# Two-layer graph network on one core: x's first tile at the head of SP's DMA queue, two x loads behind ACT's table load, one leading matmul fewer

## The chip, the cores and the metric

One core of one Trainium2 chip. The metric is the device time of one execution in microseconds; several executions are made and their median is given.

## What is computed

For each of 8 graphs there are x (1024 nodes by 256 features, float32) and a dense adjacency matrix adj (1024 by 1024). Two layers follow each other:

```python
deg = sum(adj, -1);  agg = einsum('bij,bjf->bif', adj, x) / maximum(deg, 1e-6)
x = layernorm(x + relu(concat([x, agg], 2) @ W.T))
Ah = adj + eye;  dh = rsqrt(sum(Ah, -1));  An = dh[:, :, None] * Ah * dh[:, None, :]
x = layernorm(x + relu(An @ x @ kernel + bias))
```

## The kernel before

Every matrix product is made of three TensorE products of rounded parts: each float32 operand a is split into a_hi, a rounded copy, and a_lo = a - a_hi, and hi·hi, lo·hi and hi·lo are summed in PSUM. So before TensorE can use a tile, one engine must copy it (ACT, at the start also DVE) and DVE must subtract.

The work is a loop over the 8 graphs. A graph's 1024 source nodes are 8 tiles j of 128, held on the partitions; a product gathers over j into PSUM banks 128 x 512. While one graph is worked on, the inputs of the next are loaded. SP issues nearly all loads and stores, in the order of its program, and waits only where a buffer must first come free.

The change touches only the start, before the first graph's gather. There the inputs come tile by tile:

- **SP (lines 230 to 241)** loads adj's tile 0 (`raw[:, 0, 0]`, 256 KB), adj's tile 1, and then for i = 1 to 3 a pair of x tiles (256 KB) and the two adj tiles of that pair, 256 KB each. W, the transposed x and the next rows of adj follow.
- **ACT (lines 502 to 517)** loads x's tile 0 (128 KB, `x0_loaded`) and x's tile 1 (128 KB, `x_first_loaded[0]`), loads its activation table (line 504), and then copies, in this order: the left half of adj's tile 0; x's tile 1; adj's tile 1; and for each later pair x's pair, the first adj tile, the second adj tile. Each copy waits for its own load. These copies go through one helper, so they all show line 313.
- **DVE (lines 828 to 858)** fills some constants, then copies the right half of adj's tile 0 (834), copies x's tile 0 (837), subtracts for x's tile 0 (839), for adj's tile 0 (842), for x's tile 1 (845), adj's tile 1 (847) and so on. The subtractions show line 547.
- **TensorE (`gather_start`, lines 914 to 952)** runs WARM leading matmuls on a constant tile (256 columns each, result never read), and then for each j six matmuls of 512 columns: two x_hi·adj_hi (line 936), two x_lo·adj_hi (945), two x_hi·adj_lo (949). The first two of j = 0 wait for x's tile 0 copied and both halves of adj's tile 0 copied; the next two for x's subtraction; the last two for adj's. The first two of j = 1 wait for x's tile 1 and adj's tile 1 copied, and so on. All copies run on the same in-order engines, so the order of the list above is the order in which they can be served.

In what follows adj tile 0, adj tile 1, x tile 0, x tile 1 and x pair 1 (tiles 2 and 3) are these pieces of the first graph. x pair 1 is `x[0, 1]`; before, SP loads it as its third DMA.

Of the kernel before, what the change touches and what calls it, by code (L numbers as in the profile page):

```python
# [7 lines left out]
ACT = mybir.ActivationFunctionType  # L8
# [6 lines left out]
NH = N // H  # L15
# [3 lines left out]
NB = 4  # L19
NR = 4  # L20
XP = 2
WARM = 15
LINE = 128
HALF = LINE // 8
PART = (slice(0, NH // 2), slice(NH // 2, NH))
# [4 lines left out]
def gnn_two_layers(nc, adjT, adjN, x, x_first, xT, xt_first, w, k, bias, out):  # L30
# [8 lines left out]
    with ctx:  # L39
        def sb(name, shape, dt=F32, align=32):  # L40
            return ctx.enter_context(nc.sbuf_tensor(name, shape, dt, align_bytes=align))

        def sem(name):
            return ctx.enter_context(nc.semaphore(name))

        raw = sb("adj_raw", [P, H, T, NH], F32, LINE)
        a_hi = sb("adj_hi", [P, H * T * NH], F32R, LINE)
# [9 lines left out]
        x_sb = sb("x_sb", [P, T, F])  # L57
# [23 lines left out]
        c = sb("rs_corr", [P, 2 * TH])  # L81
# [20 lines left out]
        x_first_loaded = [sem(f"x_first_loaded{h}") for h in range(H)]  # L102
        raw_first_loaded = [sem(f"raw_first_loaded{i}") for i in range(CH)]
        x_loaded = [sem(f"x_loaded{h}") for h in range(H)]
# [8 lines left out]
        x0_loaded = sem("x0_loaded")  # L113
        x0_hi_done, x0_lo_done = sem("x0_hi_done"), sem("x0_lo_done")
        adj0_left_hi, adj0_right_hi = sem("adj0_left_hi"), sem("adj0_right_hi")
# [43 lines left out]
        def xt_pair(t, i):  # L159
            return t[:, i * JC:(i + 1) * JC, :, :].rearrange("p t f c -> p (t f c)")  # L160

        def xt_source(n, first, end):
            return xT[n, first:end].rearrange("q p m -> p q m")

        def xt_target(first, end):
            return xt_pieces(xt_raw, first, end).rearrange("p (q m) -> p q m", q=end - first)

        def x_half(t, h):
            return t[:, h * TH:(h + 1) * TH, :]

        def adj_block(t, h, j, i0, n):
            at = (h * T + j) * NH + i0
            return t[:, at:at + n]
# [16 lines left out]
        def x_pair(t, i):  # L190
            return t[:, i * JC:(i + 1) * JC, :]
# [16 lines left out]
        @block.sync  # L208
        def _(sp):
            def load_adj(n, h, chunks=range(CH)):  # L210
                for i in chunks:
                    sp.dma_start(raw[:, h, i * JC:(i + 1) * JC, :],
                                 adjT[n, h, i * JC:(i + 1) * JC].rearrange("j p m -> p j m")
                                 ).then_inc(raw_loaded[h][i], 16)

            def load_x(n, h):
                pairs = CH // H
                sp.dma_start(x_half(x_sb, h).rearrange("p (i t) c -> p i (t c)", i=pairs),
                             x[n, pairs * h:pairs * (h + 1)].rearrange("i p m -> p i m")
                             ).then_inc(x_loaded[h], 16)  # L220

            def load_rows(n, t):
                i = t % NR
                sp.dma_start(nat[:, i, :], adjN[n, :, t, :]).then_inc(nat_loaded[i], 16)

            def store(b, h):
                sp.wait_ge(out_done, b * H + h + 1)
                sp.dma_start(x_half(out[b], h), x_half(x1, h)).then_inc(x1_free[h], 16)

            sp.dma_start(raw[:, 0, 0, :], adjT[0, 0, 0]).then_inc(raw_first_loaded[0], 16)  # L230
            sp.dma_start(raw[:, 0, 1, :], adjT[0, 0, 1]).then_inc(raw_loaded[0][0], 16)
            for i in range(1, CH):
                loaded = x_first_loaded[i // 2] if i % 2 == 0 else x_loaded[i // 2]
                sp.dma_start(x_pair(x_sb, i).rearrange("p t c -> p (t c)"), x[0, i]).then_inc(loaded, 16)
                sp.dma_start(raw[:, 0, JC * i, :], adjT[0, 0, JC * i]).then_inc(raw_first_loaded[i], 16)
                sp.dma_start(raw[:, 0, JC * i + 1, :],
                             adjT[0, 0, JC * i + 1]).then_inc(raw_loaded[0][i], 16)
            sp.dma_start(w_raw[:, 0], w[0]).then_inc(w_loaded[0], 16)
            sp.dma_start(xt_pair(xt_raw, 0), xt_first[0]).then_inc(xt_first_loaded, 16)
            sp.dma_start(xt_pair(xt_raw, 1), xt_first[1]).then_inc(xt0_loaded[0], 16)  # L240
            sp.dma_start(w_raw[:, 1], w[1]).then_inc(w_loaded[1], 16)
            load_rows(0, 0)
            load_adj(0, 1, [0])
            load_rows(0, 1)
            load_adj(0, 1, [1])
            for t in range(2, NR):
                load_rows(0, t)
            load_adj(0, 1, range(2, CH))
            sp.dma_start(xt_target(1, XP), xt_source(0, 1, XP)).then_inc(xt0_loaded[1], 16)
            sp.dma_start(k_raw[:], k).then_inc(k_loaded, 16)  # L250
            sp.dma_start(bias_sb[:], bias).then_inc(bias_loaded, 16)
            for t in range(NR, T):
                sp.wait_ge(deg_done, t - NR + 1)
                load_rows(0, t)

            def batch(b, more, first=False):
                if first:
                    sp.wait_ge(xt_lo_done, XP)
                    sp.dma_start(xt_target(0, XP), xt_source(1, 0, XP)).then_inc(xt_loaded, 16)
                    sp.wait_ge(resid0_done, TH // 2)  # L260
                    load_x(1, 0)
                    for h in range(H):
                        sp.wait_ge(diag_ready, h + 1)
                        load_adj(1, h)
                    sp.wait_ge(resid0_done, T // 2)
                    load_x(1, 1)
                else:
                    for h in range(H):
                        sp.wait_ge(diag_ready, b * H + h + 1)
                        load_adj(b + 1, h)  # L270
                    store(b - 1, 1)
                    for h in range(H):
                        sp.wait_ge(resid0_done, b * (T // 2) + TH // 2 * (h + 1))
                        load_x(b + 1, h)
                for t in range(NR):
                    sp.wait_ge(deg_done, b * T + NR + t + 1)
                    load_rows(b + 1, t)
                if more:
                    sp.wait_ge(xt_lo_done, b * XP + 2 * XP)
                    sp.dma_start(xt_target(0, XP), xt_source(b + 2, 0, XP)).then_inc(xt_loaded, 16)  # L280
                store(b, 0)
                for t in range(NR, T):
                    sp.wait_ge(deg_done, b * T + T + t - NR + 1)
                    load_rows(b + 1, t)

            batch(0, True, True)
            with sp.Fori(1, B - 2) as b:
                batch(b, True)
            batch(B - 2, False)
            store(B - 2, 1)  # L290
            store(B - 1, 0)
            for i, t in enumerate((T - 2, T - 1, TH)):
                sp.wait_ge(last_out_done, i + 1)
                sp.dma_start(out[B - 1, :, t, :], x1[:, t, :]).then_inc(x1_free[1], 16)
            for h in range(H):
                sp.wait_ge(x1_free[h], 16 * (B + 1 + 3 * h))
# [14 lines left out]
        def _(act):  # L311
# [187 lines left out]
                                     bias=shift16[:, q:q + 1],  # L499
                                     accum_out=moments[:, q, 1:2]).then_inc(act_var_done, 1)  # L500

            act.dma_start(x_sb[:, 0, :], x_first[0]).then_inc(x0_loaded, 16)
            act.dma_start(x_sb[:, 1, :], x_first[1]).then_inc(x_first_loaded[0], 16)
            nc.scalar.preload_act_table(ACT.Sqrt)
            act.wait_ge(raw_first_loaded[0], 16)
            copy(adj_block(a_hi, 0, 0, 0, NH // 2), raw[:, 0, 0, 0:NH // 2]).then_inc(adj0_left_hi, 1)
            act.wait_ge(x_first_loaded[0], 16)
# [37 lines left out]
        def _(dve):  # L545
            def minus(o, a, hi):
                return nc.vector.tensor_tensor(o, a, hi.bitcast(F32), ALU.subtract)  # L547
# [265 lines left out]
            def finish(b):  # L813
# [16 lines left out]
            nc.vector.memset(stats[:], 0.0).then_inc(x1_free[0], 16)  # L830
            nc.vector.memset(nb[:], 0.0).then_inc(x1_free[1], 16)
            nc.vector.memset(quarter_eps[:], LN_EPS / 4).then_inc(eps_ready, 1)
            dve.wait_ge(raw_first_loaded[0], 16)
            nc.vector.tensor_copy(adj_block(a_hi, 0, 0, NH // 2, NH // 2),
                                  raw[:, 0, 0, NH // 2:NH]).then_inc(adj0_right_hi, 1)
            dve.wait_ge(x0_loaded, 16)
            nc.vector.tensor_copy(x_hi[:, 0, :], x_sb[:, 0, :]).then_inc(x0_hi_done, 1)
            dve.wait_ge(x0_hi_done, 1)
            minus(x_lo[:, 0, :], x_sb[:, 0, :], x_hi[:, 0, :]).then_inc(x0_lo_done, 1)
            dve.wait_ge(adj0_left_hi, 1)  # L840
            dve.wait_ge(adj0_right_hi, 1)
            minus(adj_block(a_lo, 0, 0, 0, NH), raw[:, 0, 0, :],
# [42 lines left out]
        def _(pe):  # L885
# [28 lines left out]
            def gather_start():  # L914

                pe.wait_ge(warm_ready, 1)
                for _ in range(WARM):
                    nc.tensor.matmul(ring_a[:, 0, 0:F], x1s_hi[:, 0, 0:P], x1s_hi[:, 0, :],
# [194 lines left out]
```

## Time and profile before

| | |
|---|---|
| median of 3 runs | 500.82 us (500.78, 500.82, 501.29) |
| the profiled execution | 501.08 us |
| its span, first to last instruction | 499.3 us |
| TensorE matmul busy | 490.4 us (98%), 2751 matmuls |
| weight loads / DVE / ACT busy | 86% / 79% / 66% |
| DMA over the span | 93.38 MB, mean 187 GB/s |

A matmul's listed length includes its way through the array and overlaps the next one; the distance from one start to the next tells the pace. A row of the timeline gives start, length, engine, line, operation, tiles, shape and count; the part in brackets is the idle time before it and what ended that. ACTq and SPq are the instructions by which ACT and SP issue a DMA.

### The profile page before, as it was taken

What the parts mean: (1) busy time and instruction counts of PE and PEld (TensorE: products, weight loads), DVE (VectorE), ACT (ScalarE), POOL (GpSimd) and SP (SyncE); (2) the same over time, 40 slices, a digit from 0 to 9 for tenths busy, and PEclk for the clock granted to TensorE, in tenths of its full rate; (3) what the DMA queues carried; (4) which work ended last, traced back from release to release, by engine and by line L of the source; (5) the groups of instructions that cost most, each with busy time, mean ns of one, the idle gap of its engine ahead of it and who ended that gap; (6) DMA issues with size and microseconds to landing.
All of it is one profiled execution on the core that took longest, in us unless ns stands there. A gap on an engine that the chain in (4) does not pass through costs nothing.

```text
span 499.3 us, 8174 instructions
## 1 busy us (share of the span) xinstructions
PE 490.4 (98%) x2751; PEld 430.4 (86%) x2751; DVE 393.2 (79%) x963; ACT 330.6 (66%) x614; POOL 2.3 (0%) x8
## 2 busy tenths in 40 slices
PE   8999999999999999999999999999999999999993
PEld 7988888988899888998889988898888988889993
DVE  6787897679966799667996679866898668976755
ACT  6898557765766658756596574965848658477415
POOL 0000000000000000000000000000000000000001
PEclk9999999999999999999999999999999999999998
DMA  8999509762195523936149280593607932051002
GB/s 306 398 376 394 200 1 347 286 210 86 56 376 199 210 84 100 390 140 243 52 155 388 94 287 0 196 393 107 227 0 258 372 120 90 0 211 43 0 1 84
DMA packets 36878, 93.38 MB, mean 187 GB/s; under 512 B 2944, under 2 KB 3840, under 8 KB 36864
## 3 DMA queue, kind: packets, MB, share of 16 engines
q1 hardware_dynamic: 36432, 92.81, 51.1%
q10 hardware_dynamic: 432, 0.39, 0.3%
q8 instruction: 8, 0.13, 0.1%
q14 instruction: 6, 0.05, 0.0%
HBM read 84.80 MB, written 8.39 MB: 187 GB/s over the span
## 4 chain that ended last, share of the span: by engine, by line
PE 97%; ACT 1%; DMA 1%; DVE 0%; POOL 0%; issue 0%; DVEq 0%; ACTq 0%
PE ring_b L890 22%; PE ring_b L892 22%; PE ring_b L891 22%; PE ring_a L890 9%; PE ring_a L892 9%; PE ring_a L891 9%; PE ring_b L936 1%; PE ring_b L945 1%; PE ring_b L949 1%; DMA adj_raw<-adjT 1%; ACT x L381 0%; ACT adj_nat L498 0%; ACT adj_nat L495 0%; POOL x L307 0%; DVE x L678 0%
## 5 line engine op out<-in xcount | busy, mean ns | idle before, releaser
L890 PE MATMUL ring_b<-adj_hi,x1s_hi 128*128 128x512 f32 (+1 forms) x256 | 98.3, 384 | 0.0
L892 PE MATMUL ring_b<-adj_hi,x1s_lo 128*128 128x512 f32 (+1 forms) x256 | 98.0, 383 | 0.0
L891 PE MATMUL ring_b<-adj_lo,x1s_hi 128*128 128x512 f32 (+1 forms) x256 | 97.9, 382 | 0.0
L890 PE MATMUL ring_b<-adj_hi,x_hi 128*128 128x512 f32 x240 | 93.7, 391 | 0.0
L892 PE MATMUL ring_b<-adj_hi,x_lo 128*128 128x512 f32 x240 | 93.5, 390 | 0.0
L891 PE MATMUL ring_b<-adj_lo,x_hi 128*128 128x512 f32 x240 | 93.3, 389 | 0.0
L313 ACT ACTIVATE gath_hi<-ring_b 128x512 fp32r<-128x512 f32 (+1 forms) x64 | 36.5, 583 | 64.5 <-PE ring_b L892 64.5
L547 DVE TENSOR_TENSOR adj_lo<-adj_raw,adj_hi 128x1024 fp32r<-128x1024 f32 (+1 forms) x68 | 76.4, 1158 | 3.1 <-ACT adj_hi L313 3.1
L328 ACT ACTIVATE adj_nat<-adj_nat 128x1024 f32<-128x1024 f32 x64 | 67.2, 1052 | 4.9 <-DMA adj_nat<-adjN 4.6
L313 ACT ACTIVATE adj_hi<-adj_raw 128x1024 fp32r<-128x1024 f32 (+2 forms) x68 | 65.0, 997 | 1.8 <-DMA adj_raw<-adjT 1.7
L547 DVE TENSOR_TENSOR gath_lo<-ring_b,gath_hi 128x512 fp32r<-128x512 f32 (+1 forms) x64 | 42.6, 678 | 21.7 <-ACT gath_hi L313 21.7
L892 PEld LDWEIGHTS ring_b<-adj_hi,x1s_lo 128*128 128x128 f32 x256 | 48.1, 188 | 9.8
L891 PEld LDWEIGHTS ring_b<-adj_lo,x1s_hi 128*128 128x128 f32 x256 | 48.1, 188 | 8.9
L890 PEld LDWEIGHTS ring_b<-adj_hi,x1s_hi 128*128 128x128 f32 x256 | 48.1, 188 | 8.8
L892 PEld LDWEIGHTS ring_b<-adj_hi,x_lo 128*128 128x128 f32 x240 | 45.0, 188 | 9.8
L730 DVE SCALAR_TENSOR_TENSOR x1s_lo<-x,dh,x1s_hi 128x256 fp32r<-128x256 f32 x64 | 29.7, 484 | 29.6 <-ACT x1s_hi L365 29.6
L891 PEld LDWEIGHTS ring_b<-adj_lo,x_hi 128*128 128x128 f32 x240 | 45.0, 188 | 8.9
L890 PEld LDWEIGHTS ring_b<-adj_hi,x_hi 128*128 128x128 f32 x240 | 45.0, 188 | 8.8
L356 ACT ACTIVATE x<-ring_a,rdeg 128x256 f32<-128x256 f32 x64 | 27.4, 473 | 28.5 <-PE ring_a L892 14.9
L370 ACT ACTIVATE x<-x,nb,dh 128x256 f32<-128x256 f32 x64 | 36.3, 592 | 8.9 <-DVE nb L723 8.9
L603 DVE TENSOR_TENSOR x<-ring_a,x 128x256 f32<-128x256 f32 x64 | 25.4, 418 | 20.6 <-ACT x L356 20.5
L345 ACT ACTIVATE rs_root<-rs_value 128x8 f32<-128x8 f32 (+1 forms) x31 | 6.3, 204 | 51.1 <-DVE rs_value L708 51.1
(112 smaller groups left out, 966.2 us busy)
## 6 DMA issues: line engine op xcount, KB each, us to landing
adj_nat<-adjN SPq DMA_DIRECT2D x64, 512.0 KB, 5.8
adj_raw<-adjT SPq DMA_DIRECT2D x60, 512.0 KB, 9.2
out<-x SPq DMA_DIRECT2D x15, 512.0 KB, 3.3
xt_raw<-xT SPq DMA_DIRECT2D x7, 1024.0 KB, 4.8
x_sb<-x SPq DMA_DIRECT2D x14, 512.0 KB, 4.8
adj_raw<-adjT SPq DMA_DIRECT2D x8, 256.0 KB, 5.3
x_sb<-x SPq DMA_DIRECT2D x3, 256.0 KB, 5.3
x<-w SPq DMA_DIRECT2D x2, 256.0 KB, 6.3
```

What stands on the lines that cost most here:

```text
L313: return nc.scalar.activation(o, i, ACT.Copy)
L328: nc.scalar.activation(nat[:, t % NR, :], nat[:, t % NR, :], ACT.Copy, accum_out=deg[:, t:t + 1]).then_inc(deg_done, 1)
L345: nc.scalar.activation(s[:, 0:m], v[:, 0:m], ACT.Sqrt, scale=0.25).then_inc(root_done, 1)
L356: nc.scalar.activation(x1[:, t, :], ring_a[:, t % NB, F:2 * F], ACT.Copy, scale=rdeg[:, q:q + 1]).then_inc(proj0_scaled, 1)
L370: nc.scalar.activation(x1[:, t, :], x1[:, t, :], ACT.Identity, scale=dh[:, h, TH + q:TH + q + 1], bias=nb[:, q:q + 1]).then_inc(x1_done, 1)
L547: return nc.vector.tensor_tensor(o, a, hi.bitcast(F32), ALU.subtract)
L603: nc.vector.tensor_tensor(x1[:, t + o, :], ring_a[:, (t + o) % NB, 0:F], x1[:, t + o, :], ALU.add).then_inc(proj0_read, 1)
L730: nc.vector.scalar_tensor_tensor(x1s_lo[:, t, :], x1[:, t, :], dh[:, h, q:q + 1], x1s_hi[:, t, :].bitcast(F32), ALU.mult, ALU.subtract).th ...
L890: nc.tensor.matmul(o, lhi, rhi, start=(first and i == 0), stop=False)
L891: nc.tensor.matmul(o, lhi, rlo, start=False, stop=False)
L892: last = nc.tensor.matmul(o, llo, rhi, start=False, stop=last_part)
L936: nc.tensor.matmul(ring_b[:, f, :], x_at[:, f * P:(f + 1) * P], a_at, start=(j == 0), stop=False)
```

## The change

x tile 0's load moves from ACT's queue to the head of SP's. On ACT the table load comes first; behind it ACT issues x tile 1 and x pair 1, the latter taken from SP. DVE does x tile 0's copy and subtraction ahead of its half of adj tile 0. The leading matmuls are 14 instead of 15.

```diff
-WARM = 15
+WARM = 14
@@ sync
+            sp.dma_start(x_sb[:, 0, :], x_first[0]).then_inc(x0_loaded, 16)
             sp.dma_start(raw[:, 0, 0, :], adjT[0, 0, 0]).then_inc(raw_first_loaded[0], 16)
             sp.dma_start(raw[:, 0, 1, :], adjT[0, 0, 1]).then_inc(raw_loaded[0][0], 16)
             for i in range(1, CH):
-                loaded = x_first_loaded[i // 2] if i % 2 == 0 else x_loaded[i // 2]
-                sp.dma_start(x_pair(x_sb, i).rearrange("p t c -> p (t c)"), x[0, i]).then_inc(loaded, 16)
+                if i > 1:
+                    loaded = x_first_loaded[i // 2] if i % 2 == 0 else x_loaded[i // 2]
+                    sp.dma_start(x_pair(x_sb, i).rearrange("p t c -> p (t c)"), x[0, i]).then_inc(loaded, 16)
@@ scalar
-            act.dma_start(x_sb[:, 0, :], x_first[0]).then_inc(x0_loaded, 16)
+            nc.scalar.preload_act_table(ACT.Sqrt)
             act.dma_start(x_sb[:, 1, :], x_first[1]).then_inc(x_first_loaded[0], 16)
-            nc.scalar.preload_act_table(ACT.Sqrt)
+            act.dma_start(x_pair(x_sb, 1).rearrange("p t c -> p (t c)"), x[0, 1]).then_inc(x_loaded[0], 16)
@@ vector
-            dve.wait_ge(raw_first_loaded[0], 16)
-            nc.vector.tensor_copy(adj_block(a_hi, 0, 0, NH // 2, NH // 2),
-                                  raw[:, 0, 0, NH // 2:NH]).then_inc(adj0_right_hi, 1)
             dve.wait_ge(x0_loaded, 16)
             nc.vector.tensor_copy(x_hi[:, 0, :], x_sb[:, 0, :]).then_inc(x0_hi_done, 1)
             dve.wait_ge(x0_hi_done, 1)
             minus(x_lo[:, 0, :], x_sb[:, 0, :], x_hi[:, 0, :]).then_inc(x0_lo_done, 1)
+            dve.wait_ge(raw_first_loaded[0], 16)
+            nc.vector.tensor_copy(adj_block(a_hi, 0, 0, NH // 2, NH // 2),
+                                  raw[:, 0, 0, NH // 2:NH]).then_inc(adj0_right_hi, 1)
```

## Rows read from the trace of the kernel before

**Rows 1.** The page's part on the chain that ended last: shares by engine.

```profile
PE 97%; ACT 1%; DMA 1%; DVE 0%; POOL 0%; issue 0%; DVEq 0%; ACTq 0%
```

**Rows 2.** The same chain in order of time, 0 to 8 us: start us, length us, what.

```profile
0.75 3.54 DMA adj_raw<-adjT
...
4.60 0.21 DVE x_hi L837
```

**Rows 3.** Timeline of PE, matmuls, asked for in narrow windows.

```profile
1.19 3.57 PE L918 MATMUL ring_a<-x1s_hi 128*128 128x256 f32 x15 [1.19 <-DVE x1s_hi L828]
...
3.92 0.84 PE L918 MATMUL ring_a<-x1s_hi 128*128 128x256 f32 x3
4.13 0.63 PE L918 MATMUL ring_a<-x1s_hi 128*128 128x256 f32 x2
4.86 0.79 PE L936 MATMUL ring_b<-adj_hi,x_hi 128*128 128x512 f32 x1
5.45 0.63 PE L936 MATMUL ring_b<-adj_hi,x_hi 128*128 128x512 f32 x1
5.88 0.55 PE L945 MATMUL ring_b<-adj_hi,x_lo 128*128 128x512 f32 x1
6.27 0.40 PE L945 MATMUL ring_b<-adj_hi,x_lo 128*128 128x512 f32 x1
6.50 0.62 PE L949 MATMUL ring_b<-adj_lo,x_hi 128*128 128x512 f32 x2
6.96 0.61 PE L936 MATMUL ring_b<-adj_hi,x_hi 128*128 128x512 f32 x2
...
8.32 0.61 PE L936 MATMUL ring_b<-adj_hi,x_hi 128*128 128x512 f32 x2
```

**Rows 4.** Windows: window, length, busy us (count) of PE, PEld, DVE, ACT, POOL; PEclk, DMA share, GB/s.

```profile
4.86:6.08 1.22, 1.22 (x3) 1.03 (x4) 1.13 (x3) 0.57 (x2) 0.00 (x0) 1.00 1.05 306
```

**Rows 5.** Timeline, 0 to 2 us: two DMA issues on SP, one on ACT, the table load.

```profile
0.75 0.38 SPq L230 DMA_DIRECT2D adj_raw<-adjT  x1
1.19 0.42 SPq L231 DMA_DIRECT2D adj_raw<-adjT  x1
...
0.74 0.41 ACTq L502 DMA_DIRECT2D x_sb<-x_first  x1
...
1.67 1.28 ACT L504 ACT_TABLE_LOAD   x1 [1.67 <-PEq L1107]
```

**Rows 6.** Issues of DMAs in narrow windows: KB each, us from issue to landing.

```profile
x_sb<-x_first ACTq DMA_DIRECT2D x1, 128.0 KB, 3.7
...
adj_raw<-adjT SPq DMA_DIRECT2D x1, 256.0 KB, 4.1
x_sb<-x SPq DMA_DIRECT2D x1, 256.0 KB, 4.3
```

**Rows 7.** DMA of both queues up to 3.0 us, then up to 3.5 us, with SP's queue (q1).

```profile
DMA packets 150, 0.24 MB, mean 81 GB/s; under 512 B 0, under 2 KB 62, under 8 KB 150
...
DMA packets 275, 0.41 MB, mean 118 GB/s; under 512 B 16, under 2 KB 130, under 8 KB 275
...
q1 hardware_dynamic: 154, 0.30, 28.8%
```

**Rows 8.** Timeline of ACT and DVE, 4 to 8 us: copies and one subtraction.

```profile
4.31 0.42 ACT L313 ACTIVATE adj_hi<-adj_raw 128x256 fp32r<-128x256 f32 x1 [1.36 <-DMA adj_raw<-adjT]
4.52 0.29 DVE L837 CAST x_hi<-x_sb 128x256 fp32r<-128x256 f32 x1
4.84 0.42 DVE L547 TENSOR_TENSOR x_lo<-x_sb,x_hi 128x256 fp32r<-128x256 f32 x1
...
5.51 0.42 ACT L313 ACTIVATE x_hi<-x_sb 128x256 fp32r<-128x256 f32 x1 [0.79 <-DMA x_sb<-x_first]
5.83 0.61 ACT L313 ACTIVATE adj_hi<-adj_raw 128x512 fp32r<-128x512 f32 x1
...
7.01 0.63 ACT L313 ACTIVATE adj_hi<-adj_raw 128x512 fp32r<-128x512 f32 x1
```

## The prediction

> **What bounds the kernel now.** I read the chain that ended last first: TensorE's matmuls are 97% of it [rows 1]. Then the same chain at its beginning: one DMA, adj tile 0, issued at 0.75 us and landed 3.54 us later, at 4.29; then short copies; then TensorE from 4.86 on [rows 2, 3]. From 6.96 on its starts follow evenly: x tile 1's first matmul at 6.96, x pair 1's at 8.32, so six matmuls take 1.36 us, 0.227 each [rows 3]. TensorE waits for no data there. So whatever happens at the start can act in two ways only: it moves TensorE's first real matmul, or it opens a new gap in the first tiles. The change touches nothing else.
>
> The third reading is the pace. The leading matmuls start 0.21 us apart (3.92, 4.13), 256 columns each: the lower of TensorE's levels, 1.2 GHz. The first real ones have 512 columns and start 0.43 apart (5.45, 5.88); then 0.39, and from 6.27 on 0.23, the upper level, 2.4 GHz [rows 3]. The one of 0.39 ran about 0.8 at the lower pace (0.43 x 0.8 + 0.23 x 0.2 = 0.39), so the rise came at about 6.22. The granted-clock column says 1.00 for this stretch already [rows 4]; spacing and column disagree, and I go by the spacing. Before the rise TensorE had worked from 1.19 with one pause: the last leading matmul started at about 4.34 and occupied the array to 4.55, the next began at 4.86, a pause of 0.31. At the lower pace a microsecond of earlier start yields half a microsecond of work. So, with the rise fixed at 6.22, a shift of the first matmul counts half; if the rise moves along with the work, it counts whole.
>
> **The change part by part.**
>
> *x tile 0 ahead of adj tile 0 on SP's queue.* Adj tile 0 is issued one SP slot later, 1.19 in place of 0.75 [rows 5]. Does it land later? By 3.5 us both queues had moved 0.41 MB, of which SP's queue 0.30 [rows 7]; that is adj tile 0 (0.26 MB) and a little more, and on ACT's queue most of x tile 0 (0.13 MB). Its data was through shortly before 3.5 and its landing was seen at 4.29. After the change x tile 0 and adj tile 0 need the same 0.39 MB, now in sequence and not side by side. While ACT's queue is silent, adj tile 0 ends at the same moment. Lower bound 4.2 (0.02 MB less has to pass first), upper bound 4.29 + 0.44 = 4.73, the slot passed on whole. I take 4.35, near the lower end, because the sum of bytes is unchanged and x tile 1 may take a small share at the end.
>
> *x tile 0's landing.* Now 0.74 + 3.7 = 4.44 [rows 5, 6], which is the upper bound. With the queue's first 0.13 MB it should be through before 3.0, when 0.24 MB had passed [rows 7]; plus the 0.8 to 0.9 that lay between adj tile 0's last data and its landing: 3.6 to 3.9. I take 3.7.
>
> *DVE's new order.* From x tile 0's landing to the end of its subtraction now takes 4.52 to 5.26, 0.74 us [rows 8]. From 3.7 that ends at 4.46; the right half of adj tile 0 (0.29, as x tile 0's copy of the same shape) runs to 4.75. ACT's left half: 4.35 + 0.02 + 0.42 = 4.79 [rows 8]. Now the last of the three copies ends at 4.81 (x tile 0's) and TensorE starts 0.05 later. So the new start is 4.79 + 0.05 = 4.84 against 4.86: nothing. Bounds: adj tile 0 at 4.2 gives 4.69; x tile 0 at its upper bound of 4.44 gives 4.46 + 0.74 + 0.29 + 0.05 = 5.54. In microseconds of time: -0.1 to +0.3 at half weight, +0.7 at full.
>
> *x_lo and adj_lo.* x tile 0's subtraction leaves the stretch between copy and the third matmul; that matmul started at 5.88 and the subtraction ended at 5.26 [rows 3, 8]. It had 0.62 of cover already: 0.
>
> *x tile 1 and x pair 1 behind the table load.* The table load moves from 1.67 to 0.74 and takes 1.28 [rows 5]; it was covered by ACT's wait for adj tile 0 (1.36 us idle before 4.31) and still is. If ACT issues in order behind its end, x tile 1 is issued at 2.05 and x pair 1 at 2.5. Issue to landing was 3.5 for adj tile 0, 3.7 for x tile 0, and 4.3 for x tile 1 [rows 2, 6]. With 3.5, x tile 1 lands at 5.55, against 5.5 now; with 4.3, at 6.35. Who waits: ACT's copy of x tile 1 (0.32 to the next start) and behind it adj tile 1's (0.61), which now ends at 6.44, 0.52 before TensorE's j = 1 begins at 6.96. At 5.55 no wait; at 6.35 adj tile 1's copy ends at 6.37 + 0.32 + 0.61 = 7.30, a wait of 0.35. I take 0, since ACT's queue holds nothing else. x pair 1 lands at 2.5 + 4.3 = 6.8; the copy behind it, now at 7.01 to 7.64, would end near 8.1, needed at 8.32: 0, with 0.2 to spare. At 5.3 us to landing (1 us more than its row) it costs 0.8, an end for the range.
>
> *SP's queue.* One 128 KB load more at its head, one 256 KB load less in third place. Adj tile 1 is issued 0.44 later; it landed at 1.19 + 4.1 = 5.29 and ACT took it at 5.83 [rows 5, 6, 8], so even whole lateness (5.73) hides. Later loads move by less than a slot: 0.
>
> *One leading matmul fewer.* It saves 0.21 us of TensorE ahead of a wait that ends later than that anyway: 0. It widens the pause to 0.5.
>
> The sum is 0 in the profiled execution's own 501.08 us (span 499.3 plus 1.8 around it), and likewise on the median, which is 0.26 lower: 500.8.
>
> **The rivals.**
>
> *Early issue.* The table load may not hold up the DMA issues behind it, since issuing is separate from computing. Nothing in this trace shows a DMA issued behind a running ACT instruction. Then x tile 1 and x pair 1 are issued from about 0.8 and share the engines with x tile 0 and adj tile 0. Adj tile 0 is then SP's second load with a full rival queue beside it, as adj tile 1 is now: landing near 5.29 [rows 5, 6]. ACT's half gives a start at 5.29 + 0.02 + 0.42 + 0.05 = 5.78, 0.92 later. At half weight 0.46, at whole 0.92: 501.3 to 501.7, say 501.4.
> The Trainium skill (Perfetto Trace Analysis, "DVE / Act Engine Instruction") speaks for this rival: the sequencer is free for its next instruction as soon as it has pushed one into the wait queue. No row here shows it for a table load.
>
> *Late issue.* Something behind the table load could hold the issues longer. At 3.4, x tile 1 lands at 3.4 + 3.5 = 6.9, adj tile 1's copy ends at 7.85, and j = 1 begins 0.9 late: 501.7. The trace shows 1.28 for the load, then only ACT's waiting.
> The Trainium skill (ScalarE: Activation LUTs, "What ACT_TABLE_LOAD costs") has 1.28 us for the load, which rows 5 confirm, and 1.38 more for a drain, which no row shows; by an estimate from that page the issue would come at 3.4.
>
> *The other side: the clock rises later.* TensorE's pause before the first real matmul grows, from 0.31 to 0.5 in my forecast and to 1.4 with the early issue (4.34 to 5.78). If that is enough to put the rise off to the distance it had from the first leading matmul (6.22 - 1.19 = 5.03), it comes 5.03 after the first real one. Half of the stretch is lost: 2.52 in place of (6.22 - 4.86) / 2 = 0.68, so +1.8, and with the late start +2.8: 502.6 to 503.6. It decides from a rise some 2 us later than now. Against it: the pause of 0.31 did no visible harm. For it: no row shows a longer one survived.
>
> *A sooner start.* Adj tile 0 lands at 4.2 and the rise happens before the work starts: (6.22 - 4.86) / 2 + 0.1 = 0.8 less, 500.0. Nothing here can bring more, since the path into 4.86 keeps its DMA and its copy.
>
> **How the numbers follow.** The forecast has 0.50, early issue with the rise as now 0.20, late issue 0.08, the later rise 0.18, the sooner start 0.04. The runs before differ by 0.5 us, so I put 0.4 under the forecast and stretch the upper end to 502.0, which takes in both issue rivals and leaves out the later rise. The bound of 0.2% is 1.0 us, about what a measurement of this kernel can tell from no change. Faster by that needs nearly everything of the sooner start: 0.03. Slower: the later rise and a bit of the others, 0.20. Same: 0.77. The forecast's own range is 500.4 to 501.4.
>
> **What would show it.** Right: adj tile 0 lands at 4.3 to 4.4; x tile 0 near 3.7 with both its DVE steps done by 4.5; ACT's two issues at 2.05 and 2.5; first real matmul near 4.85; matmuls 0.43 apart to about 6.2; no gap at j = 1. Wrong: ACT's issues at 0.8, adj tile 0 near 5.3; or ACT's issues at 3.4 and TensorE idle before j = 1; or 0.43 spacings past 8 us.

## Result and the profile after

| | before | changed |
|---|---|---|
| median | 501.00 us (7 runs) | 502.81 us (7 runs) |
| lowest, highest | 500.78, 501.62 | 501.12, 503.78 |
| profiled execution | 501.08 | 501.12 |

The ratio is 1.0031, 95% interval 1.0022 to 1.0040: slower, by about 1.5 us by this ratio and by 1.8 between the medians, and above the upper end of the predicted range, 502.0. The profiled execution is the shortest of the seven, so its trace can't show where the median went. The change did not only shift the time, it widened it, from 0.8 us to 2.7. That was the first thing to explain.

What the trace does show is the loads. Timeline, 0 to 6 us, of the changed kernel (it answers to [rows 5] and [rows 8]):

```profile
0.74 1.28 ACT L504 ACT_TABLE_LOAD   x1 [0.74 <-PEq L1109]
...
0.75 0.38 SPq L230 DMA_DIRECT2D x_sb<-x_first  x1
0.77 0.40 ACTq L505 DMA_DIRECT2D x_sb<-x_first  x1
...
1.20 0.45 ACTq L506 DMA_DIRECT2D x_sb<-x  x1
...
3.41 0.29 DVE L836 CAST x_hi<-x_sb 128x256 fp32r<-128x256 f32 x1 [2.20 <-DMA x_sb<-x_first]
...
5.05 0.42 ACT L315 ACTIVATE adj_hi<-adj_raw 128x256 fp32r<-128x256 f32 x1 [3.03 <-DMA adj_raw<-adjT]
```

ACT issued its first load 0.03 us after the table load *began*, not behind its end at 2.02. So x tile 1 and x pair 1 were on their way from 0.77 and 1.20, beside SP's loads. The chain of the same execution, 0 to 7 us, start and length, beside [rows 2]:

```profile
1.18 3.85 DMA adj_raw<-adjT
5.03 0.02 issue
5.05 0.42 ACT adj_hi L315
5.48 0.09 issue
5.57 0.69 PE ring_b L938 x2
```

Adj tile 0 landed at 5.03 instead of 4.29, and TensorE's first real matmul began at 5.57 instead of 4.86. Yet the profiled execution lost only 0.04 us. PE's matmuls in it, against [rows 3]:

```profile
4.14 0.41 PE L920 MATMUL ring_a<-x1s_hi 128*128 128x256 f32 x1
...
5.57 0.69 PE L938 MATMUL ring_b<-adj_hi,x_hi 128*128 128x512 f32 x2 [1.02 <-ACT adj_hi L315]
...
6.10 0.63 PE L947 MATMUL ring_b<-adj_hi,x_lo 128*128 128x512 f32 x2
```

Two starts 0.53 apart (5.57, 6.10, the first with its weight load), where the kernel before took 1.02 from 4.86 to 5.88. In this execution TensorE ran at 2.4 GHz from its first real matmul on. The 0.68 us that the lower level cost before were saved, and they paid for the 0.71 of late start. The leading matmuls still started 0.21 apart up to the last one at 4.14, so the clock rose while TensorE stood idle, between 4.35 and 5.57. The question became what the clock does in the other executions.

### The profile page after: what moved, and what is told of

The parts are those of the page before. It is cut to its first block, busy times and chain, and to the rows that moved or that the text cites. A ratio compares the mean times of both kernels' runs of the same rounds, so it can differ in the third digit from the quotient of the medians.

```text
span 499.3 us, 8172 instructions
## 1 busy us (share of the span) xinstructions
PE 489.6 (98%) x2750; PEld 429.7 (86%) x2750; DVE 393.3 (79%) x963; ACT 330.5 (66%) x614; POOL 2.3 (0%) x8
## 4 chain that ended last, share of the span: by engine, by line
PE 97%; ACT 1%; DMA 1%; DVE 0%; POOL 0%; issue 0%; SPq 0%; DVEq 0%; ACTq 0%
PE ring_b L892 22%; PE ring_b L894 22%; PE ring_b L893 22%; PE ring_a L892 9%; PE ring_a L894 9%; PE ring_a L893 9%; PE ring_b L938 1%; DMA adj_raw<-adjT 1%; PE ring_b L947 1%; PE ring_b L951 1%; ACT x L383 0%; ACT adj_nat L500 0%; ACT adj_nat L497 0%; POOL x L309 0%; ACT adj_hi L315 0%
```

## The experiments

Two theories. **A:** the late data open a pause of 1.2 us in TensorE's work before the clock has risen, and in many executions the rise then comes much later. **B:** the data alone are late, and later in most executions than in the profiled one. All kernels were timed next to the kernel before; its 94 executions in all lie between 500.42 and 502.53, only three of them above 502.3.

### 1. The changed kernel again, twice

No edit. Expected of the first:

> The changed kernel once more, to see a profile of an ordinary execution; the profiled one (501.12) was the shortest of its seven. Theory A (the pause of TensorE before the first real matmul, now 1.2 us, delays the clock's rise in most executions): the first matmul again near 5.57, but in an execution of about 502.9 the spacing of 512-column matmuls stays 0.43 until 8 us or later; the whole 1.8 us over the kernel before lies before 12 us of the span. Theory B (it is the lateness of the data alone): every execution has its first matmul about 0.7 later and then waits for tiles; in an execution of 502.9 TensorE shows idle time of over 1 us between the first tiles, at a spacing of 0.23.

Measured: 501.63 (500.88 to 503.45, 11 runs); ratio 1.0014 (1.0002 to 1.0026). Its profiled execution took 502.92. PE's timeline there:

```profile
1.19 3.35 PE L920 MATMUL ring_a<-x1s_hi 128*128 128x256 f32 x14 [1.19 <-DVE x1s_hi L830]
6.02 1.19 PE L938 MATMUL ring_b<-adj_hi,x_hi 128*128 128x512 f32 x2 [1.47 <-ACT adj_hi L315]
7.01 1.05 PE L947 MATMUL ring_b<-adj_hi,x_lo 128*128 128x512 f32 x2
7.86 1.05 PE L951 MATMUL ring_b<-adj_lo,x_hi 128*128 128x512 f32 x2
8.72 0.70 PE L938 MATMUL ring_b<-adj_hi,x_hi 128*128 128x512 f32 x2
9.26 0.63 PE L947 MATMUL ring_b<-adj_hi,x_lo 128*128 128x512 f32 x2
9.72 0.62 PE L951 MATMUL ring_b<-adj_lo,x_hi 128*128 128x512 f32 x2
```

Up to 8.72 two matmuls (a pair) take 0.85, which is 1.2 GHz; from 9.26 on a pair takes 0.46, which is 2.4 GHz. The pair between took 0.54, so the clock's rise fell near 8.9. No gap lies between tiles: TensorE is never idle once it has begun. Adj tile 0 landed at 5.48 here, later again.

The second time, expected:

> The changed kernel a third time, for the distribution and a third profile. So far 18 executions: 9 from 500.9 to 501.9, 9 from 502.6 to 503.8, none between. Theory A: again two groups; a profile of the lower group has the rise before 5.6, one of the upper group near 9; adj tile 0 lands at 5.0 to 5.5 in either.

Measured: 503.48 (502.59 to 503.67, 5 runs); ratio 1.0042 (1.0029 to 1.0055). PE in its profiled execution (503.48):

```profile
5.20 1.19 PE L938 MATMUL ring_b<-adj_hi,x_hi 128*128 128x512 f32 x2 [0.65 <-ACT adj_hi L315]
...
9.61 1.05 PE L951 MATMUL ring_b<-adj_lo,x_hi 128*128 128x512 f32 x2
10.46 0.79 PE L938 MATMUL ring_b<-adj_hi,x_hi 128*128 128x512 f32 x2
```

The pair at 9.61 took 0.85 and the one at 10.46 took 0.63. The data came sooner than in either other profile (adj tile 0 at 4.67; my expectation of 5.0 to 5.5 was off), the start was only 0.34 later than before, and the execution was the longest profiled: the lower level lasted to about 10.8. That speaks against B as plainly as one trace can. Over its three sets the changed kernel has 23 executions: 9 from 500.88 to 501.90, 14 from 502.59 to 503.78 (the upper group from here on), none between. The upper group has 5 of 7, 4 of 11 and 5 of 5 executions of the three sets, and each set's median only says whether it has more than half. The first set's 502.81 is in part the luck of the draw; the second set's 501.63 would have lain below 502.0.

### 2. The pause without the change

```diff
-WARM = 15
+WARM = 11
```

on the kernel before: no DMA and no copy is touched.

> The kernel before with 11 leading matmuls in place of 15: the same DMAs and copies, the first real matmul at 4.86, but a pause of 1.2 us ahead of it. Theory A: slower by 1 to 2 us in most executions, 502 to 503, and a spread over 2 us. Theory B: unchanged, 501.0.

Measured: 502.01 (500.39 to 502.84, 7 runs); ratio 1.0018 (1.0007 to 1.0029). The profiled execution, 502.59:

```profile
1.19 2.71 PE L918 MATMUL ring_a<-x1s_hi 128*128 128x256 f32 x11 [1.19 <-DVE x1s_hi L828]
4.69 1.22 PE L936 MATMUL ring_b<-adj_hi,x_hi 128*128 128x512 f32 x2 [0.78 <-DVE x_hi L837]
...
9.12 0.90 PE L949 MATMUL ring_b<-adj_lo,x_hi 128*128 128x512 f32 x2
9.87 0.62 PE L936 MATMUL ring_b<-adj_hi,x_hi 128*128 128x512 f32 x2
```

The real work starts no later than before and still runs at the lower level until about 9.7. Leaving out work whose result nobody reads made the kernel slower. B predicted no change and fails. The run also has the shortest execution of all, 500.39. That one has no profile, but with the first profile of the changed kernel it suggests that a pause does not always delay the rise and makes the outcome depend on chance.

This run changes two things at once, since fewer leading matmuls are also less work before the data. Runs below keep the number and start the real work later. With 14, none of the 11 executions of experiment 3 is above 502.5, but 14 of the changed kernel's 23 are. With 15, one of the 94 of the kernel before is, but 4 of the 12 of experiment 6. So the number of leading matmuls alone is not the cause.

### 3. One leading matmul fewer, alone

`WARM = 14` on the kernel before.

> The kernel before with 14 leading matmuls in place of 15 and nothing else: pause 0.5 instead of 0.3. Theory A has no threshold from these runs: a pause of 1.2 costs about 1 us in the median. If the cost grows with the pause, 501.1 to 501.4; if 0.5 is still harmless, 501.0 to 501.1. Theory B: 501.0.

Measured: 500.97 (500.55 to 502.20, 11 runs); ratio 1.0001 (0.9992 to 1.0010). Its profiled execution began real work at 4.44, so adj tile 0 (ACT's copy of it began at 3.89, against 4.31) wanders by 0.4 us between executions of one kernel. Here the leading matmuls ended at about 4.34, so this execution had a pause of only 0.1, and its rise came near 5.5. The profiled execution is the shortest of its set. The removed matmul by itself costs nothing measurable.

### 4. The changed kernel with its pause filled

`WARM = 19`, then `WARM = 24`, on the changed kernel.

> The changed kernel with 19 leading matmuls, which fill the pause (the last ends near 5.4, the first real one starts at 5.57). Theory A: the clock rises during or soon after them; 501.0 to 501.4, with a spread like that of the kernel before (0.8 us). Theory B: leading matmuls do no work and the data come no sooner: unchanged, 502.8, spread 2.7 us.

> The changed kernel with 24 leading matmuls; at the lower pace they end near 6.3, so that no execution has a pause even where adj tile 0 lands at 5.5. It prices the late data alone. Theory A (late data 0.7 to 1.2 us, plus about 1.8 us for a late rise of the clock in about half of the executions): no execution of the kind of 502.8 to 503.5 is left; median 501.2 to 501.8, the start of real work bound by the leading matmuls where the rise is late. If the pause is not the cause of the upper group: about half the executions stay at 502.6 or more.

Measured: with 19, 501.65 (501.08 to 504.52, 12 runs), ratio 1.0020 (1.0008 to 1.0031); with 24, 501.56 (501.14 to 502.32, 11 runs), ratio 1.0012 (1.0003 to 1.0020). With 19 I had expected 501.0 to 501.4 and a spread of 0.8. That is a miss: one execution is at 504.52 and one at 502.68. At the lower pace 19 matmuls end near 5.4, before adj tile 0 where it lands late (5.48 and 5.63 in two profiles); it landed at 4.93 in the one profiled here (501.23), so what the long ones did is not shown. With 24 no execution is above 502.32, where the changed kernel had 14 of 23 above 502.5. Its profiled execution (501.74):

```profile
1.20 4.47 PE L920 MATMUL ring_a<-x1s_hi 128*128 128x256 f32 x24 [1.20 <-DVE x1s_hi L830]
6.16 0.70 PE L938 MATMUL ring_b<-adj_hi,x_hi 128*128 128x512 f32 x2 [0.49 <-ACT adj_hi L315]
6.71 0.63 PE L947 MATMUL ring_b<-adj_hi,x_lo 128*128 128x512 f32 x2
```

24 matmuls in 4.47 us, where 14 took 3.35: the clock rose among them, near 4.3. So they ended near 5.5, and a pause of 0.6 followed after all, which my expectation had ruled out. It came after the rise, and the first pair behind it took 0.55, the pace of 2.4 GHz. Adj tile 0 landed as late as 5.63, and the median is 0.60 above the kernel before beside it (500.96). That 0.6 us is a net price: in the profiled execution the start is 1.30 later, and the low stretch of 0.68 is saved.

### 5. Why adj tile 0 is late

Three kernels each change who shares the DMA engines with it. First, ACT's loads held until a small ACT copy behind the table load is done (`table_done` is a new semaphore):

```diff
             nc.scalar.preload_act_table(ACT.Sqrt)
+            act.wait_ge(eps_ready, 1)
+            copy(shift[:, 0:1], quarter_eps[:]).then_inc(table_done, 1)
+            act.wait_ge(table_done, 1)
             act.dma_start(x_sb[:, 1, :], x_first[1]).then_inc(x_first_loaded[0], 16)
```

> The changed kernel with the two DMA issues of ACT held until a small ACT copy behind the table load is done, so that they are issued near 2.3 instead of 0.77 and 1.20; 14 leading matmuls. If adj tile 0 was late because ACT's two loads shared the DMA engines with it, it lands at 4.2 to 4.5 instead of 5.03 and the first real matmul starts at 4.7 to 5.0. Theory A: pause 0.4 to 0.6, time 500.8 to 501.5. Theory B: 500.8 to 501.2. If the load was late because it is the second of its queue, adj tile 0 still lands near 5.0 and the time stays at 502 to 503.

Measured: 502.68 (502.14 to 503.43, 5 runs); ratio 1.0035 (1.0022 to 1.0048). This is nearly the kernel that my forecast had in mind (its issues come 0.2 later than the forecast's 2.05 and 2.5), and it is no better. The timeline of ACT in it:

```profile
2.04 0.20 ACT L316 ACTIVATE shift<-quarter_eps 128x1 f32<-128x1 f32 x1
2.27 0.39 ACTq L509 DMA_DIRECT2D x_sb<-x_first  x1
...
3.93 0.42 ACT L316 ACTIVATE adj_hi<-adj_raw 128x256 fp32r<-128x256 f32 x1 [1.69 <-DMA adj_raw<-adjT]
6.23 0.42 ACT L316 ACTIVATE x_hi<-x_sb 128x256 fp32r<-128x256 f32 x1 [1.89 <-DMA x_sb<-x_first]
```

The timeline of PE in the same execution:

```profile
4.45 1.20 PE L942 MATMUL ring_b<-adj_hi,x_hi 128*128 128x512 f32 x2
...
7.32 0.70 PE L942 MATMUL ring_b<-adj_hi,x_hi 128*128 128x512 f32 x2 [0.62 <-ACT adj_hi L316]
...
10.06 0.70 PE L942 MATMUL ring_b<-adj_hi,x_hi 128*128 128x512 f32 x2 [1.12 <-ACT adj_hi L316]
```

Adj tile 0 landed at 3.9 and real work started at 4.45, as this theory of sharing says; the rise was near 5.8. But x tile 1 landed only at 6.2 and x pair 1 later still (6.06 us after its issue at 2.69), and TensorE stood 0.6 us before tile 1 and 1.1 before tile 2. Both theories' figures for the time missed this.

Second, x pair 1 back on SP's queue:

> The changed kernel with x pair 1 back in SP's queue, so that ACT's queue carries x tile 1 alone; 14 leading matmuls. Theory A: adj tile 0 shares the DMA engines with x tiles 0 and 1 only, as in the kernel before, and lands at 4.2 to 4.5; first matmul 4.7 to 5.0; 500.8 to 501.4. If the place behind x tile 0 in SP's queue is the harm: adj tile 0 still near 5.0 and 502 to 503.

Measured: 501.39 (500.94 to 502.50, 11 runs); ratio 1.0008 (0.9999 to 1.0017). Adj tile 0 landed at 4.47, real work started at 5.01 after a pause of 0.66, and the rise came near 6.6. No execution is above 502.5.

Third, adj tile 0 ahead of x tile 0 again, all else as changed, DVE in its old order:

```diff
-            sp.dma_start(x_sb[:, 0, :], x_first[0]).then_inc(x0_loaded, 16)
             sp.dma_start(raw[:, 0, 0, :], adjT[0, 0, 0]).then_inc(raw_first_loaded[0], 16)
+            sp.dma_start(x_sb[:, 0, :], x_first[0]).then_inc(x0_loaded, 16)
```

> The changed kernel with adj tile 0 ahead of x tile 0 in SP's queue and DVE in the old order; x tile 1 and x pair 1 stay on ACT's queue, 14 leading matmuls. If the place behind x tile 0 costs a slot (the run with x pair 1 back on SP had 4.48 against 3.9 to 4.3), adj tile 0 lands at 4.0 to 4.4 here, x tile 0 at 4.3 to 4.8, first real matmul 4.8 to 5.2, pause 0.5 to 0.8; 501.0 to 501.6 and few executions above 502.5. If it is only the sharing with ACT's queue, adj tile 0 is still at 5.0 or later and two groups remain.

Measured: 501.10 (500.75 to 503.31, 12 runs); ratio 1.0010 (0.9997 to 1.0022). Adj tile 0 landed at about 4.0 (ACT took it at 4.05), though x pair 1 stayed on ACT's queue. But x tile 0 came at 4.7, so the start was at 5.08, after a pause of 0.7, and 3 of 12 executions are at 503.1 to 503.3. TensorE also started tile 2 at 8.54 where 8.12 would have followed, because the first adj tile of that pair landed only at 7.75.

The moved x pair 1 by itself, on the kernel before, as ACT's third load:

> The kernel before with one part of the change alone: x pair 1 is ACT's third load (behind x tiles 0 and 1) instead of SP's third. Theory A (ACT's loads share the DMA engines with adj tile 0 while it comes in; x pair 1 is the one that was not there before): adj tile 0's bytes go in beside x tiles 0 and 1 as before and only their tail meets x pair 1, so it lands at most 0.3 later than 4.29, first real matmul 4.9 to 5.2, time 501.0 to 501.5. If x pair 1 on ACT's queue is the whole harm: adj tile 0 near 5.0, 502 to 503.

Measured: 500.92 (500.53 to 501.92, 11 runs); ratio 1.0000 (0.9991 to 1.0009). ACT took adj tile 0 at 4.17, real work started at 4.72. So neither part alone makes the lateness. Adj tile 0 lands at 3.9 behind x tile 0 with nothing beside it (loads held, and everything on SP, experiment 7); at 4.47 behind x tile 0 with x tile 1 beside it; at 4.0 when it is first with x tile 1 and x pair 1 beside it; and at 4.67 to 5.63 behind x tile 0 *and* with both beside it, in five profiles. The first three rest on one or two profiles each, and 4.47 is only 0.2 from the five, so it could be scatter; 3.9 and 4.0 are further away.

### 6. The two reorderings alone

The kernel before with the table load ahead of ACT's two issues, and DVE's x tile 0 ahead of its half of adj tile 0.

> The kernel before with the two reorderings of the change and none of its moved loads: ACT's table load ahead of its two DMA issues, and DVE's copy and subtraction of x tile 0 ahead of its half of adj tile 0. ACT's issues should still be at 0.77 and 1.2 (a table load does not hold them). x tile 0 lands near 4.4 here, at the same time as adj tile 0, so DVE's half comes 0.7 later: first real matmul at 5.2 to 5.5, pause 0.6 to 0.9, 501.2 to 501.8. If the first matmul stays below 5.0: x tile 0 lands earlier than in the kernel before.

Measured: 501.59 (500.79 to 503.56, 12 runs); ratio 1.0021 (1.0009 to 1.0032). DVE and ACT's queue:

```profile
0.77 0.40 ACTq L503 DMA_DIRECT2D x_sb<-x_first  x1
...
3.84 0.42 ACT L313 ACTIVATE adj_hi<-adj_raw 128x256 fp32r<-128x256 f32 x1 [1.82 <-DMA adj_raw<-adjT]
...
4.02 0.29 DVE L834 CAST x_hi<-x_sb 128x256 fp32r<-128x256 f32 x1 [2.82 <-DMA x_sb<-x_first]
4.35 0.43 DVE L547 TENSOR_TENSOR x_lo<-x_sb,x_hi 128x256 fp32r<-128x256 f32 x1
4.70 0.28 DVE L838 CAST adj_hi<-adj_raw 128x256 fp32r<-128x256 f32 x1
```

The table load again does not delay the issue behind it. DVE's half of adj tile 0, landed by 3.84, waited behind x tile 0's two steps until 4.70; the start was at 5.12 after a pause of about 0.6, and 4 of 12 executions are at 502.76 or more. The profiled one (500.79) is the shortest of its set, at 2.4 GHz from the start of real work; none of the four was profiled. In the changed kernel this order is harmless, because x tile 0 is there at 3.4.

### 7. Everything on SP

```diff
@@ sync
             sp.dma_start(raw[:, 0, 0, :], adjT[0, 0, 0]).then_inc(raw_first_loaded[0], 16)
+            sp.dma_start(x_sb[:, 1, :], x_first[1]).then_inc(x_first_loaded[0], 16)
             sp.dma_start(raw[:, 0, 1, :], adjT[0, 0, 1]).then_inc(raw_loaded[0][0], 16)
```

on the changed kernel (an excerpt), with no load on ACT and x pair 1 back on SP. It was meant to beat both.

> All first loads on SP: x tile 0, adj tile 0, x tile 1, adj tile 1, x pair 1 and so on, none on ACT; 14 leading matmuls. The run with held issues had adj tile 0 at 3.91 and the first matmul at 4.45, but x tile 1 only at 6.2. Theory A: here adj tile 0 lands at 3.9 to 4.0, first matmul at 4.45 to 4.55 with no pause behind the leading ones, x tile 1 before 5.2 and no gap at the second tile: 0.2 to 0.4 faster than the kernel before, 500.4 to 500.9, with a small spread. Theory B (lateness of the data alone): the same 0.3 to 0.4 faster. If one queue alone can't feed the engines: x tile 1 or adj tile 1 after 5.8 and a gap at the second or third tile, 501 or more.

Measured: 501.95 (500.88 to 502.64, 11 runs); ratio 1.0020 (1.0011 to 1.0029): slower. PE in its profiled execution:

```profile
4.43 1.19 PE L936 MATMUL ring_b<-adj_hi,x_hi 128*128 128x512 f32 x2
...
6.84 0.63 PE L936 MATMUL ring_b<-adj_hi,x_hi 128*128 128x512 f32 x2
...
9.03 0.70 PE L936 MATMUL ring_b<-adj_hi,x_hi 128*128 128x512 f32 x2 [0.63 <-ACT adj_hi L315]
```

Real work began at 4.43, about as expected, with hardly a pause (0.1). But TensorE then stood before tile 2 for a copy that waited for its load. Its load is adj tile 2's: it was issued at 3.07 where the kernel before issued it at 2.12, and landed at 8.23. The start won 0.4 us; the stand cost 0.8 (8.22, where the next pair would have followed, to 9.03); and the rise, near 6.5 in place of 6.22, made the low stretch longer by 0.7, which costs 0.36. No tried version beats the kernel before.

## Why the prediction was wrong

A profiled execution can be added up from three readings of PE's timeline: the first real matmul's start, against 4.86; half of the stretch from there to the rise (the low stretch), against 0.68; and the gaps between tiles, each counted from where the next pair would have followed to where it started.

| execution | start | low stretch, half | gaps | sum against before | measured against 501.08 |
|---|---|---|---|---|---|
| changed, first profile | +0.71 | 0 | 0 | +0.03 | +0.04 |
| changed, second | +1.16 | 6.02 to 8.9, 1.44 | 0 | +1.92 | +1.84 |
| changed, third | +0.34 | 5.20 to 10.8, 2.80 | 0 | +2.46 | +2.40 |
| changed, 24 leading | +1.30 | 0 | 0 | +0.62 | +0.66 |
| before, 11 leading | -0.17 | 4.69 to 9.7, 2.51 | 0 | +1.66 | +1.51 |
| x pair 1 back on SP | +0.15 | 5.01 to 6.6, 0.80 | 0 | +0.27 | +0.26 |
| ACT's loads held | -0.41 | 4.45 to 5.8, 0.68 | 0.78 + 1.29 | +1.66 | +1.84 |
| everything on SP | -0.43 | 4.43 to 6.5, 1.04 | 0.81 | +0.74 | +0.81 |

So nearly the whole difference lies ahead of 11 us, and the method of the prediction, start shift plus half of the low stretch, holds to 0.15 us where no gap lies between tiles; with gaps the sum comes out up to 0.2 short. What failed are the values put in.

- **ACT's issues behind the table load.** The step "x tile 1 is issued at 2.05 and x pair 1 at 2.5" failed: 0.77 and 1.20. Early issue had 0.20 against 0.50 for the forecast. The rule of the Trainium skill (Perfetto Trace Analysis, "DVE / Act Engine Instruction"), that the sequencer goes on once it has pushed an instruction, agrees with this: in all eight traces with the table load in front and nothing between, the issue came at 0.77. The drain of 1.38 us that the Trainium skill (ScalarE: Activation LUTs, "What ACT_TABLE_LOAD costs") adds to the table load does not show here: the held copy began at 2.04, 0.02 after the table load's end.
- **Adj tile 0 at 4.35** failed for the same reason: 4.67 to 5.63, and 3.91 once the two issues were held. That 3.91 lies below the lower bound of 4.2 too, so "adj tile 0 ends at the same moment" was wrong in the other direction as well. The early-issue rival had 5.29 and a start at 5.78; the three starts are 5.20, 5.57 and 6.02. Its mechanism was right. Its price of +0.5 is near the 0.6 with 24 leading matmuls, partly by luck: the rival had the rise fixed at 6.22, and there it was near 4.3.
- **The issues held after all would not have given 500.8.** The wait of 0 at tile 1 went with 3.5 us from issue to landing, and x tile 1 took 3.9 from its issue at 2.27; x pair 1 took 6.06 where I took 4.3. The slack of 0.5 us at tile 1 and of 0.2 at tile 2 was too thin for that.
- **x tile 0** landed at 3.4 where I had 3.7, and DVE's new order cost nothing in this kernel, as forecast. **One leading matmul fewer** cost nothing alone, as forecast.
- **The later rise** decided the median. It had 0.18, as an outcome of its own; it is rather a coin toss in each execution, once the pause is there. Priced 502.6 to 503.6, the upper group lies at 502.59 to 503.78, with 14 of 23 executions. Part of that agreement is luck: the rival put the rise 5.03 behind the first real matmul, and it came 5.6 and 5.0 behind it in two profiles (third of the changed kernel, 11 leading) but only 2.9 in the second of the changed kernel, where a start later than priced made up for it. The argument against it, that a pause of 0.31 did no harm, said nothing of one of 1.2; the price took in the late start, but the chance should have been a share of early issue's, since the first creates the pause of the second.

Shown: a longer pause, made without touching the loads, slows the kernel (experiment 2); at an equal number of leading matmuls a later start brings the upper group (experiments 3 and 6); and when the leading matmuls run on past the rise the upper group is gone (experiment 4, 24 of them). Argued only: that the upper group's executions are all late rises. Two of the 14 were profiled, and both are. Left open: from which length a pause begins to hurt. Groups above 502.5 appear with pauses of 0.6 (4 of 12) and 0.7 (3 of 12), not with 0.66 in another kernel (0 of 11), so the length alone doesn't settle it. The rise also moves with hardly a pause (0.1): with the same 14 leading matmuls and real work from 4.43 to 4.45 on, it came near 5.5, 5.8 and 6.5 in three kernels. Open too are the 504.52 and the 502.68 with 19 leading matmuls.

## What to carry to other kernels

Leading matmuls that bridge to the first data are worth only what the bridge is worth in its worst execution: in this kernel they had to reach past the clock's rise or to the latest landing, not the usual one, and a pause before the rise was a risk of some 1 to 2 us (0.8 to 2.1 in the three profiles with a late rise), not only idle time. A DMA issue placed behind ACT's table load is not behind it in time (0.77 against an end at 2.02); a wait on a semaphore that a copy behind the load sets did hold it (2.27). And where a profiled execution is the shortest of its set, take another profile before explaining the median with it.

## What the runs showed of the hardware that was not expected

- The table load takes 1.28 us on ACT, and a DMA issue behind it in ACT's program starts 0.03 us after its beginning.
- The moment of TensorE's rise to 2.4 GHz differs between executions of one kernel: before 5.6, near 8.9 and near 10.8 us in three profiles of the changed kernel, all with the same leading matmuls from 1.2 to 4.4. With 24 leading matmuls it came near 4.3.
- The column of the granted clock does not show the lower level at the start. In the second profile of the changed kernel it stands at 1.00 for a stretch of matmuls 0.43 apart (windows: length, busy us and count by engine, PEclk, DMA share, GB/s):

```profile
6.02:8.70 2.68, 2.68 (x6) 2.12 (x7) 2.18 (x5) 2.08 (x5) 0.00 (x0) 1.00 0.97 371
9.30:12.00 2.70, 2.70 (x13) 2.21 (x12) 2.70 (x6) 2.60 (x5) 0.00 (x0) 1.00 1.06 402
```

  Six matmuls in 2.68 us against thirteen in 2.70 (one of them begun before the window) tell the two levels apart; the column doesn't.
- A load's landing at the start wanders by 0.8 us in one and the same kernel: adj tile 0 took 3.5, 3.85 and 4.30 us from its issue in the three profiles of the changed kernel. With 24 leading matmuls, the same loads, it took 4.4.
